# A two-row LSTM on one core: most of x*Wx moved from the prologue into the loop

## The reference

```python
x = x + _L0_cond_ref(x, cond, weight)        # a modulated 256x256 projection
x = x + _L1_cond_ref(x, cond, Wx, Wh, b)     # an LSTM over 1024 steps, state 256

xW = jnp.einsum('ntd,dk->tnk', x, Wx) + b    # 4 gates of 256
def step(carry, xw_t):
    a = xw_t + prev_h @ Wh
    i, f, o = sigmoid(a[:, :H]), sigmoid(a[:, H:2*H]), sigmoid(a[:, 2*H:3*H])
    g = tanh(a[:, 3*H:])
    next_c = f * prev_c + i * g
    next_h = o * tanh(next_c)
```

## Time and profile before

| | |
|---|---|
| median of 3 runs | 2076.16 us (2069.64 to 2078.4) |
| profiled execution, its own time | 2075.25 us |
| its span, first to last instruction | 2073.5 us |
| mean granted TensorE clock | 0.521 of full speed |
| TensorE busy (matmuls) | 90% of the span |
| VectorE busy | 61% |
| ScalarE busy | 33% |
| GpSimd busy | 24% |

### The profile page before, as it was taken

How to read it: one execution, slowest core, us unless ns; L and a number is a source line. 1 busy time by engine, 2 the same in 40 slices (tenths; PEclk the granted TensorE clock), 3 DMA queues, 4 the chain that set the end, 5 groups by cost and what they waited for, 6 DMA issues and landing times.

```text
span 2073.5 us, 140158 instructions
## 1 busy us (share of the span) xinstructions
PE 1876.1 (90%) x57580; PEld 1735.6 (84%) x57580; DVE 1269.7 (61%) x8384; ACT 689.4 (33%) x4125; POOL 498.7 (24%) x1291
## 2 busy tenths in 40 slices
PE   9999999999999999999999999999999999999997
PEld 5588888888888888888888888888888888888887
DVE  3366666666666666666666666666666666666665
ACT  2233333333333333333333333333333333333333
POOL 1122222222222222222222222222222222222221
PEclk9855555555555555555555555555555555555555
DMA  2000000000000000000000000000000000000000
GB/s 86 2 1 1 1 1 1 1 1 1 1 1 1 1 1 1 1 1 1 1 1 1 1 1 1 1 1 1 1 1 1 1 1 1 1 1 1 1 1 1
DMA packets 20368, 6.67 MB, mean 3 GB/s; under 512 B 17532, under 2 KB 19848, under 8 KB 20360
## 3 DMA queue, kind: packets, MB, share of 16 engines
q1 hardware_dynamic: 20088, 6.30, 1.2%
q10 hardware_dynamic: 272, 0.26, 0.0%
HBM read 4.46 MB, written 2.10 MB: 3 GB/s over the span
## 4 chain that ended last, share of the span: by engine, by line
PE 75%; DVE 10%; ACT 9%; issue 5%; DMA 0%; SPq 0%; POOLq 0%; POOL 0%; DVEq 0%
PE psum L295 75%; DVE psum L586 10%; ACT scan_in L663 9%; PE psum L318 0%; DMA small_rows<-in_L_cond_b_dram 0%; ACT xw L642 0%; DVE w L468 0%; SPq L185 0%; POOLq L56 0%; PE psum L300 0%; POOL y_cols L246 0%; DVE y_rows L600 0%; DVE y_rows L605 0%; DVE h_parts L589 0%; DVE ys L464 0%
## 5 line engine op out<-in xcount | busy, mean ns | idle before, releaser
L295 PE MATMUL psum<-h_parts,wh_p 128*128 128x2 f16 (+1 forms) x45056 | 1370.4, 166 | 0.0
L295 PEld LDWEIGHTS psum<-h_parts,wh_p 128*128 128x128 f16 x45056 | 1286.5, 104 | 16.2
L295 PE MATMUL psum<-ring,ident_b 128*128 128x4 bf16 (+2 forms) x12288 | 491.2, 168 | 186.2 <-DVE psum L586 184.7
L295 PEld LDWEIGHTS psum<-ring,ident_b 128*128 128x128 bf16 x12288 | 407.4, 105 | 271.0 <-DVE psum L586 268.6
L660 ACT ACTIVATE sig_f<-psum 128x4 f32<-128x4 f32 x1024 | 178.3, 174 | 1127.1 <-DVE psum L577 1127.1
L577 DVE TENSOR_REDUCE psum<-psum 128x4 f32<-128x8 f32 x1024 | 178.9, 175 | 389.2 <-PE psum L295 389.2
L234 POOL CAST ring<-xw 128x64 bf16 (+1 forms) x256 | 120.7, 471 | 1148.5 <-POOLq L272 1124.0
L589 DVE SCALAR_TENSOR_TENSOR h_parts<-scan_h 128x4 f16<-128x4 f32 x1024 | 175.9, 172 | 247.7 <-ACT scan_h L667 247.7
L665 ACT ACTIVATE scan_h<-psum 128x4 f32<-128x4 f32 x1024 | 180.2, 176 | 142.2
L592 DVE TENSOR_TENSOR_SCAN h_parts<-scan_h,h_parts 128x12 f16<-128x12 f32 x1024 | 188.0, 184 | 35.1
L579 DVE TENSOR_REDUCE psum<-psum 128x4 f32<-128x8 f32 x1024 | 179.1, 175 | 39.7
(11 more groups left out here) (74 smaller groups left out, 155.9 us busy)
## 6 DMA issues: line engine op xcount, KB each, us to landing
out_dram<-y_rows SPq DMA_DIRECT2D x512, 4.0 KB
x_rows<-in_x_dram SPq DMA_DIRECT2D x4, 512.0 KB, 6.9
wh_sb<-in_L_cond_Wh_dram SPq DMA_DIRECT2D x1, 1024.0 KB, 10.2
wx_sb<-in_L_cond_Wx_dram SPq DMA_DIRECT2D x1, 1024.0 KB, 11.9
w_sb<-in_L_cond_weight_dram ACTq DMA_DIRECT2D x1, 256.0 KB, 2.8
small_rows<-in_cond_dram SPq DMA_DIRECT2D x1, 2.0 KB
small_rows<-in_L_cond_b_dram SPq DMA_DIRECT2D x1, 4.0 KB
```

Source lines behind the costliest of these rows:

```text
L295: return nc.tensor.matmul(out_, lhs, rhs, start=first, stop=last, skip_group_check=True)
```

## The change

**Prologue.** Only the first `LEAD` = 17 of the 128 items of x*Wx are made there. An item is one chunk m, one batch row and one block of 128 steps, so 16 items cover the first 128 steps; each is two float32 matmuls of 128 columns, read out by VectorE. `xw` is laid out by items. Wx gets a maximum, scales and two float16 parts of its own (`wx_p`), as Wh has. VectorE splits steps 128 to 271 of x into three bfloat16 parts (`x_p`). The second half of the first layer is done last.

**Loop, TensorE.** In each turn one more item is made, from `wx_piece` (256 x 128 of Wx, two parts) and `x_piece` (256 x 128 of x, three parts): 12 matmuls of 128 columns, two in each of steps 2 to 7. The input of gate f is put in before the wait for `c_done`, and waits for `f_act` instead; one of the two matmuls follows it. The other stands after the input of gate o, before the wait for `h_hi`. The 12th signals `x_mm`.

**Loop, ScalarE.** After step 7's tanh it reads the finished item out of `X_BANK` into `xw` (`x_read`).

**Loop, SyncE.** After `x_split` and `x_mm` of a turn it copies the next turn's `wx_piece` and `x_piece` within SBUF (`stage`), and then waits for `y_turned` and stores as before. TensorE waits for both copies (`x_staged`) in step 2.

**Loop, GpSimd.** The split is cut in pieces, each behind a wait for a further row of h (`calm_after`); a turn's first half also makes the three parts of 8 more steps of x in four operations of 32 elements a partition (`x_split`).

```diff
+FIRST_PIECE = 2
+LEAD = 17
+AHEAD = 2 * LEAD
...
+        xw = sb("xw", [P, NI, P])
+        wx_p = sb("wx_p", [P, 2, K, G * D], F16)
+        x_p = sb("x_p", [P, 3, K, B, T], BF16)
+        wx_piece = sb("wx_piece", [P, 2, K, P], F16)
+        x_piece = sb("x_piece", [P, 3, K, P], BF16)
...
+            def stage(turn):
...
+                    item = sp.snap((turn + LEAD) % NI)
+                    weights = sp.snap(((item // B) % M) * P)
+                    rows = sp.snap((item % B) * T + (item // ITEMS) * P)
+                sp.dma_start(wx_piece[:, :, :, :].rearrange("p w k n -> p (w k) n"),
+                             wx_p[:, :, :, bass.ds(weights, P)].rearrange("p w k n -> p (w k) n")).then_inc(x_staged, 16)
+                sp.dma_start(x_piece[:, :, :, :].rearrange("p q k n -> p (q k) n"),
+                             x_p[:, :, :, :, :].rearrange("p q k b t -> p (q k) (b t)")[:, :, bass.ds(rows, P)]).then_inc(x_staged, 16)
...
+            stage(0)
+            with sp.Fori(0, NI - 1) as i:
+                sp.wait_ge(x_split, i + 2)
+                sp.sem_inc(store_seen, 1)
+                sp.wait_ge(x_mm, i + 1)
+                sp.sem_inc(store_seen, 1)
+                stage(i + 1)
                 sp.wait_ge(y_turned, i + 2)
                 sp.sem_inc(store_seen, 1)
...
+            def calm_after(step):
+
+                pool.wait_ge(h_all, step)
+                pool.sem_inc(pool_seen, 1)
...
+                pool.wait_ge(x_read, i + 1)
+                pool.sem_inc(pool_seen, 1)
                 for half in range(2):
+                    done = t + (half + 1) * HALF
+                    src = xw_source(half, i + 1)
                     pool.wait_ge(ring_used, 1)
                     pool.sem_inc(ring_used, -1)
-                    split(half, t + UNROLL + half * HALF)
-                    pool.wait_ge(h_all, t + (half + 1) * HALF)
-                    pool.sem_inc(pool_seen, 1)
+                    calm_after(done)
+                    split_high(half, src)
+                    split_rest(half, src)
+                    calm_after(done + 1)
                     if half == 0:
                         pool.wait_ge(y_turned, i + 1)
                         pool.sem_inc(pool_seen, 1)
                     save(half, t + half * HALF)
+                    split_middle(half)
+                    calm_after(done + 2)
+                    split_low(half)
+                    if half == 0:
+                        nc.gpsimd.tensor_copy(part[0], now).then_inc(s_pool, 1)
+                        settle()
+                        calm_after(done + 3)
+                        nc.gpsimd.tensor_tensor(res, now, part[0], ALU.subtract).then_inc(s_pool, 1)
+                        settle()
+                        nc.gpsimd.tensor_copy(part[1], res).then_inc(s_pool, 1)
+                        settle()
+                        nc.gpsimd.tensor_tensor(part[2], res, part[1], ALU.subtract).then_inc(x_split, 1)
...
-            for n in range(NB):
-                for s, v in last_read("x1", n):
-                    pe.wait_ge(s, v)
-                for b in range(B):
-                    for m in range(M):
-                        bank = start_group(("xw", b, m, n))
-                        for k in range(K):
-                            last = mm(bank[:, :], wx_sb[:, k, m * P:(m + 1) * P], xt[:, k, b, n * BANK:(n + 1) * BANK], k == 0, k == K - 1)
-                        last.then_inc(s_filled, 1)
+            for v in range(LEAD):
+                block, m, b = v // ITEMS, (v // B) % M, v % B
+                bank = start_group(("xw", v))
+                for k in range(K):
+                    last = mm(bank[:, 0:P], wx_sb[:, k, m * P:(m + 1) * P], xt[:, k, b, block * P:(block + 1) * P], k == 0, k == K - 1)
+                last.then_inc(s_filled, 1)
+            for n in range(1, NB):
+                project_x(n, range(B))
...
+                terms = [(k, w_part, x_part) for k in range(K) for w_part in range(2) for x_part in range(3)]
+
+                def project(n):
+
+                    k, w_part, x_part = terms[n]
+                    return mm(banks[X_BANK][:, 0:P], wx_piece[:, w_part, k, :], x_piece[:, x_part, k, :], n == 0, n == len(terms) - 1)
...
+                    if u == FIRST_PIECE:
+                        pe.wait_ge(x_staged, 32 * i + 32)
+                        pe.wait_ge(x_read, i + 1)
+                    pe.wait_ge(f_act, t + u + 1)
+                    input_apart(GATE_F, u, 0, K)
+                    if u >= FIRST_PIECE:
+                        project(done)
+                        done += 1
                     pe.wait_ge(c_done, t + u + 1)
-                    input_apart(GATE_F, u, 0, K)
                     input_apart(GATE_G, u, 0, K)
...
+                    if u >= FIRST_PIECE:
+                        last = project(done)
+                        done += 1
+                        if done == len(terms):
+                            last.then_inc(x_mm, 1)
                     pe.wait_ge(h_hi, t + u + 1)
...
+                    if u == UNROLL - 1:
+
+                        act.wait_ge(x_mm, i + 1)
+                        act.sem_inc(act_seen, 1)
+                        nc.scalar.activation(xw[:, bass.ds(item, 1), :].rearrange("p n t -> p (n t)"), banks[X_BANK][:, 0:P], ACT.Identity,
+                                             bias=bias_s[:, bass.ds(chunk, 1)], scale=x_unit[:, :]).then_inc(x_read, 1)
```

More of the change, by code:

```diff
@@ L51, in cond_resid_lstm @@
     NI = T // UNROLL
+    ITEMS = M * B
+    assert NI == (T // P) * ITEMS and LEAD == ITEMS + 1 and ITEMS & (ITEMS - 1) == 0 and NI & (NI - 1) == 0 and B == 2
     NB = T // BANK
@@ L157, in cond_resid_lstm @@
             groups += per_bank("xt", n)
-        groups += per_bank("x1", 0) + [(("wmax",), "dve")]
+        groups += per_bank("x1", 0) + [(("wmax",), "dve"), (("h0wh",), "dve"), (("scales",), "dve")]
+        groups += [(("xw", v), "dve") for v in range(LEAD)]
         for n in range(1, NB):
             groups += per_bank("x1", n)
-        groups += [(("scales",), "dve"), (("h0wh",), "dve")]
-        groups += [(("xw", b, m, n), "act" if m % 2 else "dve") for n in range(NB) for b in range(B) for m in range(M)]
         order = {what: g for g, (what, _) in enumerate(groups)}
@@ L198, in _, with store @@
             sp.sem_inc(s_out, 2 * 16 * stores)
-            with sp.Fori(0, NI) as i:
+            def stage(turn):
+                if isinstance(turn, int):
+                    item = (turn + LEAD) % NI
+                    weights, rows = ((item // B) % M) * P, (item % B) * T + (item // ITEMS) * P
+                else:
+                    item = sp.snap((turn + LEAD) % NI)
[5 more added lines that the diff above has]
+                             x_p[:, :, :, :, :].rearrange("p q k b t -> p (q k) (b t)")[:, :, bass.ds(rows, P)]).then_inc(x_staged, 16)
+            def store(turn):
+                for q in range(stores):
+                    sp.dma_start(out_t[q, :, bass.ds(turn * (UNROLL * K), UNROLL * K), :],
+                                 y_rows[q * QUAD:(q + 1) * QUAD, :]).then_inc(s_out, 16)
+            sp.wait_ge(s_wx_hi, 1)
+            sp.wait_ge(s_wx_lo, 1)
+            sp.wait_ge(x_split, 1)
+            stage(0)
[5 more added lines that the diff above has]
+                stage(i + 1)
                 sp.wait_ge(y_turned, i + 2)
                 sp.sem_inc(store_seen, 1)
-                for q in range(stores):
-                    sp.dma_start(out_t[q, :, bass.ds(i * (UNROLL * K), UNROLL * K), :],
-                                 y_rows[q * QUAD:(q + 1) * QUAD, :]).then_inc(s_out, 16)
+                store(i)
+            sp.wait_ge(y_turned, NI + 1)
+            store(NI - 1)
             sp.wait_ge(s_out, 16 * stores * (NI + 2))
@@ L336, in _ @@
             pe.wait_ge(s_wy, B * K)
-            project_x(0)
+            project_x(0, range(B))
             bank = start_group(("wmax",))
[L340 to L348, removed]
+            pe.wait_ge(s_wmax, 2)
+            nc.tensor.transpose(bank[0:1, 0:P], wmax[:, 0:1], ident[:, :])
+            nc.tensor.transpose(bank[0:1, P:2 * P], wmax[:, 1:2], ident[:, :]).then_inc(s_filled, 1)
             bank = start_group(("h0wh",))
@@ L522, in _ @@
+            bank = group(("h0wh",))
+            nc.vector.tensor_copy(h0wh[:, :, :], bank[:, 0:M * B].rearrange("p (m b) -> p m b", b=B)).then_inc(s_dve, 1)
             bank = group(("scales",))
-            nc.vector.tensor_copy(scales[:, :], bank[:, 0:2]).then_inc(s_dve, 1)
+            nc.vector.tensor_copy(scales[:, :], bank[:, 0:4]).then_inc(s_dve, 1)
             dve.wait_ge(*read_out(order[("scales",)]))
```

152 lines of the change are left out of this document (96 added, 56 removed).

## The result

The changed kernel takes 2141.08 us (median of 4 runs, 2139.21 to 2143.2) where the kernel before takes 2076.39: a ratio of 1.0318, 95% interval 1.0292 to 1.0343. The profiled execution took 2139.21 us, 64.0 more than before's 2075.25. The forecast was 2159, slower.

A forecast was written before the change was run, and what follows sets the result against it. It took one recurrence to bound the kernel, its last-ending chain 75% TensorE. From 2075.25 us, minus 43.6 for the prologue, plus 127 for late copies and 0.9 for the median, it forecast 2159 us, whole range 2026 to 2250.

The forecast's parts named there:

- The mechanism and the sign: Staging copies reach TensorE too late for step 2 of each turn, making the kernel slower; chance of slower 0.63.
- Its size: Lateness of the staged pieces before step 2: 1.0 us a turn, +127 us over 127 turns.
- split of x done: GpSimd's splitting of x ends 2.13 us after T7, when step 7's identity loads may start; bounds 1.85 and 2.9.
- pitch: On SyncE, from the first staging copy's issue to the second's: 0.82 us, read from the stores.
- to landing: From the second staging copy's issue to its data's arrival: 2.8 us, bounds 2.0 and 4.3.
- The prologue: Fewer input projections before the loop save 43.6 us, so the loop starts at 45 us instead of 88.6.
- The projections hidden: In the loop, both 128-column matmuls of a step, 0.107 us each, fit TensorE's idle stretches: 0 us.
- GpSimd's order gains nothing: In the loop, cutting GpSimd's split into pieces has no contention with VectorE to remove: 0 us.
- The rule on pieces under 512 bytes: For the x_piece copy's 256-byte pieces: perhaps 0.4 us more per landing, 51 us in all, left out of the sum.
- in time: Rival: the staging copies land before step 2 needs them, giving 2032 us; chance 0.27.
- The clock: Rival: TensorE's granted clock rises in the loop, 45 us less: 1987 or 2114 us; chance 0.06.
- The second matmul: Rival: a step's second 128-column matmul isn't hidden, up to +71 us, 2230; within the late case's 0.60.

The follow-up runs named there:

- e1: The changed kernel with SyncE waiting for x_split of the turn before (i + 1 for i + 2): 2024.57 us, ratio 0.9783.
- e2: The changed kernel without GpSimd's wait for the fourth row of h (calm_after(done + 3)): 2024.59 us, ratio 0.978.
- e3: The changed kernel with the copy of x_piece made as two, so three copies a turn: 2199.03 us, ratio 1.0627.
- e4: The changed kernel with the two copies in exchanged order, x_piece first and wx_piece second: 2087.79 us, ratio 1.0087.
- e7: e1 with both matmuls of a step's pair before the wait for the cell: 2024.47 us, ratio 0.9776.
- e8: e1 with added 128-column matmuls into an unused bank, 384 columns in every step: 2029.43 us, ratio 0.9797.
- e6: e1 with both matmuls of a step's pair after the input of gate o: 2075.25 us, ratio 1.0015.
- e5: e1 without all of GpSimd's waits for further rows of h, its order as before the change: 2039.08 us, ratio 0.9846.
- e10: e5 with only the wait for the half's last row of h put ahead of the split's four operations: 2037.36 us, ratio 0.9834.
- e11: The kernel before the change with only GpSimd's waits for further rows of h added: 2087.99 us, ratio 1.0082.
- e9: The changed kernel without GpSimd's waits for further rows of h, SyncE still waiting for this turn's x_split: 2042.14 us, ratio 0.9854.

## Why the prediction was right, point by point

- **The mechanism and the sign** were right: the pieces are late in each turn, TensorE stands in front of step 2, the next turn is late anew. e1 and e2 take the lateness away from either end and both land at 0.978; e3 and e4 move it by +0.49 and -0.40 us a turn, and the time follows by 63 and -48 us, 127 turns' worth.
- **Its size** was 1.0 us a turn, measured 0.87. Term by term (forecast, then measured from the rows of after): split of x done T7+2.13, 2.09; from there to the first issue 0.85, 0.52; pitch 0.82, 1.10; to landing 2.8, 2.6; landed T7+6.6, 6.31. The two terms on SyncE's queue are both off, by -0.33 and +0.28, and that they nearly cancel is luck: its register instructions cost less ahead of the first copy (0.21 us of them) and more ahead of the second (0.26, where my pitch was that of the stores). It was due at T7+5.6 by my count and, as 6.31 - 0.87 shows, at 5.44. TensorE starts 0.26 after the landing where I allowed 0.05, then needs 0.45 to the first Wh load where I had 0.51, and the group that follows is 0.07 longer, which I had left out.
- **The prologue** was to give 43.6 us and gave 46.2. The 68 short records took 9.5 us busy for 8.2, so of the 5.1 us that I had counted for VectorE on the way only 1.2 are left: its passes run beside TensorE's work, which goes on without a break from 10 to 39.8 us.
- **The projections hidden**: right for both slots (e7, e8, and the 1.93 us of the changed kernel's other steps), except in the late step, where the pair is on the path. The upper bound of 0.22 us for a 128-column matmul is ruled out by e6.
- **GpSimd's order gains nothing**: this step was wrong in its reason. I inferred from before's unlengthened operations that there was no contention between GpSimd and VectorE. There is (e5, e10, e11); before's phase happened to keep clear of it by some hundredths of a microsecond. In e5 the phase is another, and then the waits are worth 13 to 14.5 us (e5 against e1). The likely reason, argued and not isolated, is the register arithmetic that the changed kernel adds ahead of GpSimd's cast: 0.05 us of it in the kernel before, single instructions of up to 0.23 in e5. Their other effect, to hold `x_split` back past step 7, costs 111 us in the changed kernel; undoing them alone (e9) is worth 96 us net. The sum was unhurt, because before and the changed kernel both have unlengthened scans: the right 0 for a wrong reason.
- **The rule on pieces under 512 bytes** (the Trainium skill, DMA: Bandwidth & Descriptors, Specifications) doesn't show here: 768 pieces of 256 bytes, 192 KB, landed in 2.6 us, where 256 pieces of 1 KB from the chip's memory took 2.8. Further down, under Why small descriptors are slow (HBM only), the same page takes copies within SBUF, as these are, out of the penalty for small pieces. The 0.4 us that the prediction tried for it came from no row.
- The rivals: *in time* is what e1 makes, 2024.6 against before's 2069.8, a gain of 45 us where 43.6 was forecast. *The clock* stayed at 0.50, with more columns too (e8). *The second matmul* is hidden.

e1, e2 and e7 are the versions to keep, all at 0.978 of the kernel before.

## What to carry to other kernels

A wait on a counter should ask for what the data needs: here the copy needed the split of the turn before, and asking for this turn's put a chain of four links (h's row, GpSimd, SyncE, the copy) inside a window of 5.4 us. Price such a chain from the signal to the wake-up, with each register instruction and issue on the way, before the work that it feeds. And when an engine's operations show no mark of contention, look at how far apart in phase they are; a new wait or a few register instructions can move them onto each other.

## What the runs showed of the hardware

- A VectorE scan with two SBUF inputs and a GpSimd subtraction collide as if one holds what the other needs until it ends: the scan ended 0.05 us after the subtraction in e5 and in e11, and lost overlap minus 0.14 us each time (0.25 of overlap cost 0.11, 0.21 cost 0.07, and 0.07 cost nothing in the kernel before). That agrees with the Trainium skill (SBUF — State Buffer, SBUF: two separate sides), which calls the port pair of the two engines an exclusive lock, taken by VectorE operations with two SBUF inputs and held for the whole instruction.
- With a GpSimd cast in the subtraction's place the rows don't agree with "the whole instruction". In e10 a scan that starts 0.02 us after the cast is lengthened by 0.07, but ends 0.20 before the cast does; and in the kernel before, the high part of h, which also reads two operands from SBUF, starts 0.19 after the cast L238 did, runs wholly under it and takes its 0.17. It looks as if a cast is in the way at its start alone.
- The collision with a subtraction would explain one more row of the changed kernel's prologue, VectorE's and GpSimd's timelines:

```profile
33.33 3.13 DVE L673 SCALAR_TENSOR_TENSOR xw<-h0wh,scales,xw 128x16 f32<-128x16 f32 x1
```

```profile
32.33 4.08 POOL L322 TENSOR_TENSOR wx_p<-wx_s,wx_p 128x2048 f16<-128x2048 f32 x1
```

  An operation on 16 elements lasts 3.13 us, until 36.46, while GpSimd's long subtraction ends at 36.41. It costs nothing, as TensorE is at the first layer's second half until 39.8. That this is the cause was not tried by an experiment of its own.
- A 128-column matmul of 2-byte operands at 1.2 GHz takes about 0.1 us of the stream (an estimate from e6's 0.066 us a step).
- SyncE needs 0.93 to 1.10 us from one copy with a computed address to the next, of which 0.7 is the issue itself and 0.14 to 0.26 the register instructions ahead of it (e4, the changed kernel); with these at 0.05 the pitch is 0.8 (e3).
